# Dequantising products over 24 rows instead of 128, and a new order of the first loads, in a half-step feed-forward, Mamba and gated-MLP kernel

## The reference

```
x = x + 0.5 * ffn(layernorm(x))                 # quantised linear, with LoRA
x = x + attn(layernorm(x))                      # rmsnorm, Mamba2 scan, gated MLP 512 -> 1792 -> 512
x = x + 0.5 * ffn(layernorm(x))                 # the same quantised linear again

def ffn(x):                                     # q is int 0..15, one scale and one zero per group of 64
    W = (q - zeros) * scales                    # 512 x 512, 8 groups along the input
    return x @ W.T + (x @ lora_A.T) @ lora_B.T / 16 + bias
```

## Time and profile before

| | |
|---|---|
| median of 3 runs | 756.31 us (755.76 to 756.35) |
| the profiled execution, its own time | 755.21 us |
| its span, first to last instruction | 753.5 us |
| TensorE busy in it | 737.6 us |
| VectorE, ScalarE, GpSimd busy | 642.2, 456.1, 345.1 us |
| TensorE's granted clock, mean | 0.997 of full |
| first product of the Mamba part starts | 40.88 us into the span |

### The profile page before, as it was taken

How to read it: one execution, slowest core, us unless ns; L and a number is a source line. 1 busy time by engine, 2 the same in 40 slices (tenths; PEclk the granted TensorE clock), 3 DMA queues, 4 the chain that set the end, 5 groups by cost and what they waited for, 6 DMA issues and landing times.

```text
span 753.5 us, 10656 instructions
## 1 busy us (share of the span) xinstructions
PE 737.6 (98%) x3424; PEld 360.2 (48%) x3424; DVE 642.2 (85%) x1257; ACT 456.1 (61%) x895; POOL 345.1 (46%) x391
## 2 busy tenths in 40 slices
PE   8999999999999999699999999999999999999998
PEld 3444455555555565344444444444444444444444
DVE  7799999889989988978899977977977978767994
ACT  4868888787787785345546456357456456444441
POOL 5631455665453478786423243243242243224574
PEclk9999999999999999999999999999999999999999
DMA  8943656474432224250612734734734633434474
GB/s 304 198 77 70 167 102 123 115 141 99 98 85 43 44 70 107 61 112 1 154 28 39 172 56 86 167 56 84 167 59 78 161 71 71 84 70 77 117 170 140
DMA packets 98790, 77.67 MB, mean 103 GB/s; under 512 B 65600, under 2 KB 73088, under 8 KB 98736
## 3 DMA queue, kind: packets, MB, share of 16 engines
q0 software_dynamic: 17280, 31.46, 23.5%
q1 hardware_dynamic: 78592, 41.01, 21.1%
q10 hardware_dynamic: 2864, 4.52, 2.3%
HBM read 24.77 MB, written 5.54 MB: 40 GB/s over the span
## 4 chain that ended last, share of the span: by engine, by line
PE 70%; DVE 19%; ACT 4%; issue 3%; DMA 3%; POOL 2%; SPq 0%; ACTq 0%; POOLq 0%; DVEq 0%
PE PS L2298 62%; DVE stage L1686 2%; DVE st L1508 1%; PE PS L2436 1%; DMA x_t<-hb 1%; DVE S L1643 1%; DVE raw L1686 1%; DVE h2n_p L1599 1%; PE PS L2428 1%; PE PS L2394 1%; DVE xs L1607 1%; DVE w_in L1790 1%; PE PS L2412 1%; PE PS L2386 1%; PE PS L2421 1%
## 5 line engine op out<-in xcount | busy, mean ns | idle before, releaser
L2298 PE MATMUL PS<-h,w_in 128*128 128x512 f16 x480 | 108.1, 379 | 0.5 <-DMA h<-hn_p 0.5
L2298 PE MATMUL PS<-h,x_t 128*128 128x512 f16 x408 | 95.3, 383 | 3.7 <-DVE pre L2122 3.5
L790 POOL DMA_DIRECT2D xs<-x x42 | 36.7, 880 | 92.1 <-ACT x L1371 88.9
L2298 PEld LDWEIGHTS PS<-h,w_in 128*128 128x128 f16 x480 | 46.4, 98 | 62.1 <-issue 11.1
L2298 PE MATMUL PS<-n_T,stage 128*128 128x512 f16 x288 | 71.5, 379 | 0.0
L2298 PEld LDWEIGHTS PS<-h,x_t 128*128 128x128 f16 x408 | 39.6, 99 | 52.8 <-issue 6.5
L1371 ACT ACTIVATE x<-PS,d_d 128x512 f32<-128x512 f32 x59 | 40.2, 682 | 39.5 <-PE PS L2298 38.7
L586 POOL TENSOR_TENSOR r<-mv,mhalf 128x1 f32<-128x1 f32 (+1 forms) x32 | 28.9, 902 | 53.4 <-DVE mv L1512 38.7
L1341 ACT ACTIVATE xds<-tm,dgh 128x512 f32<-128x512 f32 x24 | 17.3, 722 | 53.3 <-DVE tm L2222 53.3
L2298 PE MATMUL PS<-pre,stage 128*128 128x512 f16 x192 | 49.3, 379 | 0.0
L2298 PEld LDWEIGHTS PS<-n_T,stage 128*128 128x128 f16 x288 | 28.2, 98 | 34.0 <-ACT x L1371 0.3
(11 more groups left out here) (349 smaller groups left out, 1911.7 us busy)
## 6 DMA issues: line engine op xcount, KB each, us to landing
xs<-x POOLq DMA_DIRECT2D x58, 256.0 KB, 3.3
xs<-n POOLq DMA_DIRECT2D x21, 256.0 KB, 3.3
xl<-x POOLq DMA_DIRECT2D x17, 256.0 KB, 3.3
x_t<-x_in SPq DMA_DIRECT2D x16, 256.0 KB, 3.5
x_t<-hb POOLq DMA_DIRECT2D x16, 256.0 KB, 4.7
out<-x_t SPq DMA_DIRECT2D x15, 256.0 KB, 2.3
raw_gu<-gate_t SPq DMA_DIRECT2D x7, 512.0 KB, 4.5
raw_gu<-up_t SPq DMA_DIRECT2D x7, 512.0 KB, 6.4
```

The source lines that it names most:

```text
L790: po.dma_start(end_row(c), d_tmps[d % 3], accum_op=ALU.add).then_inc(s_acc[d % 3], 16)
L2298: ins = pe.matmul(out_, lhs(a, b, k), rhs(a, b, k), start=first and n == 0, stop=last and n == len(todo) - 1)
```

## The change

- `R_LORA` goes from 32 to 8, so that the 8 group rows and the 16 LoRA rows lie together. The products of `ffn_parts` read only 8 rows (scales) and 24 rows (the other). Nothing else of the three tiles is read, and the four fills go: three on VectorE, one on GpSimd, with their semaphores and the waits on them.
- SP issues the scales and `lora_b_t` first, then x0, q0, x1, q1, q2, q3, bias, x2, x3. Before, it was x0, q0, scales, `lora_b_t`, q1, x1, bias, q2, q3, x2, x3.
- VectorE: `clear()` and `zero_rows()` now stand ahead of `prep0(0, 0)`.
- TensorE: 7 idle products instead of 9, and `ffn_parts(3)` ahead of `first_t0(1)`.

```
-N_WARM = 9
+N_WARM = 7
-        R_LORA = 32
+        R_LORA = NG
+        N_ROWS = NG + RANK
...
+            sp_.dma_start(sc[0:NG, :], scales_t).then_inc(s_la, 16)
+            sp_.dma_start(w_rows[R_LORA:N_ROWS, :], lora_b_t).then_inc(s_la, 16)
             load_x(0, 0)
             load_q(0)
-            sp_.wait_ge(e_wzero, 1)
-            sp_.dma_start(sc[0:NG, :], scales_t).then_inc(s_la, 16)
-            sp_.wait_ge(e_wzero, 2)
-            sp_.dma_start(w_rows[R_LORA:R_LORA + RANK, :], lora_b_t).then_inc(s_la, 16)
+            load_x(1, 1)
             load_q(1)
-            load_x(1, 1)
-            sp_.dma_start(hb[:, :], bias.broadcast_to([P, DM])).then_inc(s_hb, 16)
             load_q(2)
             load_q(3)
+            sp_.dma_start(hb[:, :], bias.broadcast_to([P, DM])).then_inc(s_hb, 16)
...
-            rows = sel_rows[0:R_LORA, :].rearrange("p (k r) -> p k r", k=KB)
-            po.memset(sel_rows[32:64, :], 0.0).then_inc(e_szero, 1)
+            rows = sel_rows[0:NG, :].rearrange("p (k r) -> p k r", k=KB)
...
-            ac.wait_ge(e_szero, 1)
-            ac.dma_start(sel_rows[R_LORA:R_LORA + RANK, :], lora_a).then_inc(s_la, 16)
+            ac.dma_start(sel_rows[R_LORA:N_ROWS, :], lora_a).then_inc(s_la, 16)
...
-            ve.memset(sc[:, :], 0.0).then_inc(e_wzero, 1)
-            ve.memset(w_rows[:, :], 0.0).then_inc(e_wzero, 1)
-            ve.memset(sel_rows[64:P, :], 0.0).then_inc(e_wzero, 1)
...
                 ve.wait_ge(s_la, 64)
-                ve.wait_ge(e_wzero, 2)
...
+            clear()
+            zero_rows()
             prep0(0, 0)
-            zero_rows()
-            clear()
             ffn_weight(0)
...
-                pe.matmul(bank(s_), sel_rows[:, cols], sc[:, :], start=True, stop=True)
+                pe.matmul(bank(s_), sel_rows[0:NG, cols], sc[0:NG, :], start=True, stop=True)
...
-                pe.matmul(bank(z), sel_rows[:, cols], w_rows[:, :], start=True, stop=True).then_inc(e_parts, 1)
+                pe.matmul(bank(z), sel_rows[0:N_ROWS, cols], w_rows[0:N_ROWS, :], start=True, stop=True).then_inc(e_parts, 1)
...
             pe.wait_ge(s_la, 64)
-            pe.wait_ge(e_wzero, 3)
             pe.wait_ge(e_tab, 1)
             ffn_parts(0)
             ffn_parts(1)
             pe.wait_ge(e_tab, 2)
             first_t0(0)
             ffn_parts(2)
+            ffn_parts(3)
             first_t0(1)
-            ffn_parts(3)
             first_f(0)
```

More of the change, by code:

```diff
@@ L289, in build @@
         e_max = sem("e_max"); e_maxT = sem("e_maxT"); e_max1 = sem("e_max1"); e_all = sem("e_all"); e_wsum = sem("e_wsum"); e_scale = sem("e_scale"); e_whi = sem("e_whi"); e_wlo = sem("e_wlo"); e_small = sem("e_small"); e_fhi = sem("e_fhi"); e_flo = sem("e_flo")
-        e_tab = sem("e_tab"); e_zero = sem("e_zero"); e_wzero = sem("e_wzero"); e_szero = sem("e_szero"); e_zs = sem("e_zs")
+        e_tab = sem("e_tab"); e_zero = sem("e_zero"); e_zs = sem("e_zs")
         e_aexp = sem("e_aexp"); e_wf = sem("e_wf"); e_dve = sem("e_dve"); e_pool = sem("e_pool")
```

## The result

The changed kernel takes 763.24 us (median of 4, 760.04 to 763.48) against 756.03 for the kernel before on the same chip: 1.0081 times as long, 95% interval 1.0061 to 1.0100. It is 7 us slower; forecast were 755.9 us and no change. The profiled execution, at 760.04 us with a span of 758.2, is the fastest of the four.

What follows compares the result with a forecast made beforehand. TensorE, busy 737.6 of 753.5 us, was taken as the bound, its start set by the bias-transfer chain to the residual. Saving 0.45 us less 0.05 for the clock gave 756.31 - 0.4 = 755.9 us, range 754.3 to 757.6.

Steps and rivals of the forecast that it cites:

- the start of the products: TensorE's `ffn_parts(0)` starts at 4.3 us, 1.5 earlier; after 0.6 lost to the clock, net 1.0 us earlier (0.5 to 1.4).
- rival 3: TensorE's clock stays at its lower level through the short products; residual waits 2.8 to 6.2 us, say 761 us; chance 0.13.
- signs named for being wrong: 0.85 us passes beyond 8 us, `lora_a` after 5, `proj(0, 0)` not waiting for transposed chunks, or a second stretch at clock 0.5.
- Array rows: On TensorE, 0.1 us for each change between full and short products; hidden weight loads uncertain, at worst 16 of some 0.1 us.
- VectorE: VectorE free by 2.9 us either way, fills cost nothing; chunk 0 normalised at 7.9 instead of 6.46, covered with 0.4 to spare.
- Bias: Bias load, now behind q2 and q3, lands between 9.8 and 11.0 us; 0.1 us lost, so `xb(0)` is issued 0.9 earlier.
- Its transfer: GpSimd's DMA adding the bias to chunk 0, 7.1 us before; half of the 0.9 us gain kept, 0.45 us.
- two readings: Bias transfer either takes a fixed 7.1 us and keeps all 0.9 us, or waits for w_in's drain and keeps nothing.
- Clock at the start: TensorE's clock rises at 5.5 us again, so 1.2 us of products run at half pace and 0.6 is lost (0.2 to 0.75).
- The 20.5 us behind the residual: Work from the residual at 20.36 to `proj(0, 0)` at 40.88 keeps its order and length, so any earlier residual shifts it.
- forecast of no change: 755.9 us, counted as the same since under about 0.2% (1.5 us) cannot be told apart; chance of same 0.67.
- The saving of 0.4 us: Total for the whole kernel: 0.45 us off the residual and the end, less 0.05 for a possible longer clock stretch.

Runs made afterwards that it cites:

- x5_warm16: The changed kernel with 16 idle products instead of 7; 761.32 us, ratio 1.0077.
- x11: The changed kernel with each of its eight short products replaced by one over all 128 rows of a zero tile; 756.44 us, ratio 1.0004.
- x8: The kernel before with the change's order, seven idle products, fills spread over two engines and products over 128 rows; 756.02 us, ratio 1.0007.
- x3: The kernel before with its nine idle products over 8 rows instead of 128; 757.63 us, ratio 1.0030.
- x9_after_again: The changed kernel run again without any edit, for a second profile; 762.50 us, ratio 1.0092.
- x12: The changed kernel with its short products replaced by ones over 8 and 24 rows of a zero tile; 762.02 us, ratio 1.0078.
- x1_rows_only: The kernel before with only its block products cut to 8 and 24 rows, fills, waits and order kept; 764.10 us, ratio 1.0109.

## Why the prediction was wrong

**The step that failed** stands in the start of the products: "If it rises at 5.5 again, 1.2 us of the new products run at half pace and 0.6 is lost." It took the clock's rise to depend on time and on TensorE being occupied, and let it hold from there. The short products do neither. In one profile the clock was up when they began and nothing was lost at first, but it fell after 3.3 us of them and TensorE went 13.6 us at the lower level; in the other it went there for everything up to 22.8 us, instead of 1.2 us. This was rival 3, with a chance of 0.13 and 759 to 762.5 us. Its price for the residual nearly held: `first_f(0)` would end between 23.1 and 26.5 and the residual with it; it was 22.89 in one profile and 25.30 in the other. Its time was a little low, since the median is 763.24: it charged only the residual's wait, and what moved `proj(0, 0)` was TensorE's whole stream, 4.06 us where the residual was 2.53 late. What argued against it there, that all full-row passes ran at the upper level, bore only on full-row passes. The honest reading was that no row of the trace showed a stretch of products over few rows at all, and such a gap deserved a larger chance. Three of the signs named for being wrong are in the profile: passes of 0.85 us beyond 8 us, a further stretch at 0.50, and a `proj(0, 0)` that no longer waits for a transposed chunk.

**Start of the products.** Foretold 4.3, was 4.28. The last small load came at 3.4, not 4.2; the idle products set the start, not the loads.

**Array rows.** Hidden weight loads are confirmed (x5_warm16). The changes of form were a little under-priced: 0.1 us holds for going out of the short form, going in took 0.25, so a pair is 0.34 and not 0.2.

**VectorE.** It was free at 2.75 (2.9 foretold) and then waited for `lora_a` until 3.43, so the fills' own time cost nothing, as foretold. Chunk 0 was later than reckoned (statistics at 5.16, held 1.05 us by its load behind the small ones), still ahead of TensorE.

**Bias.** Halved at 10.29 with no wait for its load: the 0.1 us of leak was 0.

**Its transfer.** I took half of two readings. The one of a nearly fixed time was right: 7.2 us after an issue at 12.11, 6.8 after 12.94 in x11, 7.0 after 14.58 and 14.72 in x8 and x3. The term was mis-sized, 0.45 us where 1.0 was there.

**Clock at the start.** In x11, with rows taken out of the question, the first four passes took 3.17 us (4.20 to 7.37) instead of 4 x 0.43 = 1.72, so 1.45 us and not 0.6 were lost to the lower level. The bias transfer was then issued only 0.23 us earlier than before, not 0.9, and took 6.8 us instead of 7.1. That the residual came 0.49 us early, forecast 0.45, is luck.

**The 20.5 us behind the residual** are not rigid. "A shift of the whole stream moves the end" holds for a delay (x3_idle8: 1.5 us late, 1.9 us longer) but not for 0.5 us of gain, which SP's queue of transposes took back. Without the rows the forecast of no change would have been right. The saving of 0.4 us (a ratio of 0.9995) is neither seen nor excluded: x11's is 1.0004, interval 0.9992 to 1.0015.

## What to carry to other kernels

Cutting a product's contraction rows does not shorten it (0.86 us from one to the next at the upper level, over 24 rows as over 128), and can double the time of all products around it: at 48 rows and fewer this kernel's clock fell to the lower level, or stayed there, while TensorE was busy without a gap, and zero rows in the operands, filled while loads are under way anyway, were the cheaper way. When a change makes products smaller, look for a stretch of such products in the old trace; if there is none, run one alone before trusting the cost. Read TensorE's pace from the starts of its passes, since a busy share of 98% and an empty idle column look the same at either level, and the granted clock was printed as 1.00 over 13.6 us at half pace in x9_after_again.

## What the runs showed of the hardware

- A fall of the granted clock without idleness: 13.60 us at 0.50, busy for 13.60. The Trainium skill, TensorE: Matmul & The Clock Gate, Part 1, describes the gate as following how busy TensorE has been. The rows here differ from that reading: busy time alone did not hold or release it, and with everything else the same the number of array rows decided (x11 and x12, 756.44 and 762.02 us).
- Nine idle products over 8 rows of a zero tile had not raised the clock by 5.83 us (x3_idle8). The same nine over 128 rows had in the profiles of the kernel before (by 5.81) and with 64 and 96 rows, but not in that of x1_rows_only, where short products began at 5.56; sixteen of them had in x5_warm16. All of them are on zeros, so zeros do not keep it down.
- GpSimd's accumulating transfer took 6.8 to 7.3 us from issue to landing whenever it was issued between 12.1 and 14.7 us. In the changed kernel its first packets came about 4 us after the issue, between 16.0 and 16.5 us, while w_in's queue had taken 101 to 103% of the engines from 12 to 16 us.
